# Six tiles instead of seven turned and added by DMA in a residual GNN kernel, the seventh on TensorE, with writes, loads and GpSimd's scaling in another order

## What is computed

```python
x = layernorm(x + gnn_with_batchnorms(x, adj))       # two linear layers, batch statistics
h = relu(adj @ (x @ Wg0 + bg0))                      # per batch
h = relu(adj @ (h @ Wg1 + bg1))
for p in (1, 2, 3, 4):                               # windows of p rows of the 128
    wins = h[:, :nw * p, :].reshape(B * nw, p, H)    # nw = 128 // p
    last = lstm_last(Wih[p-1], Whh[p-1], bih[p-1], bhh[p-1], wins)
    h = h.at[:, arange(nw) * p + (p - 1), :].set(last.reshape(B, nw, H))
x = layernorm(x + h)
```

## Time and profile before

| what | value |
|---|---|
| median of 3 runs | 751.12 us (750.57 to 752.2) |
| the profiled execution, its own time | 748.24 us |
| span of its profile | 746.4 us |
| TensorE's granted clock over the span | 0.995 |
| TensorE, VectorE, ScalarE, GpSimd busy | 97%, 86%, 72%, 42% |

### The profile page before, as it was taken

The page is one execution under the profiler, slowest core; times in us unless marked ns, Lnnn a source line. Parts: engine busy times, 40 slices in busy tenths (PEclk is TensorE's granted clock), DMA queues, the critical chain, the costliest instruction groups (busy, mean ns, idle before and its releaser), DMA issues.

```text
span 746.4 us, 11167 instructions
## 1 busy us (share of the span) xinstructions
PE 726.6 (97%) x3828; PEld 414.8 (56%) x3828; DVE 644.1 (86%) x1379; ACT 540.2 (72%) x882; POOL 315.2 (42%) x289
## 2 busy tenths in 40 slices
PE   8999999999999999998999999999999999999894
PEld 6777544677777776773444444444444444554442
DVE  6888787899998989857998788899998888888987
ACT  4878998567777776748887787777767766676582
POOL 1000000168788787810000001028287385996286
PEclk9999999999999999999999999999999999999998
DMA  5643400024424233113400006051743526519012
GB/s 158 187 139 97 113 1 0 1 62 109 113 58 114 70 101 89 55 29 146 192 1 2 0 11 117 0 101 50 134 109 74 119 51 141 142 28 215 27 57 84
DMA packets 95291, 61.56 MB, mean 82 GB/s; under 512 B 25178, under 2 KB 94212, under 8 KB 94212
## 3 DMA queue, kind: packets, MB, share of 16 engines
q1 hardware_dynamic: 87844, 49.84, 23.7%
q0 software_dynamic: 7392, 11.01, 7.5%
HBM read 27.55 MB, written 16.78 MB: 59 GB/s over the span
## 4 chain that ended last, share of the span: by engine, by line
PE 60%; DVE 21%; ACT 7%; DMA 4%; SPq 3%; issue 3%; POOL 0%; POOLq 0%; DVEq 0%
PE ps L739 8%; PE ps L740 8%; PE ps L748 8%; PE ps L707 7%; PE ps L744 5%; PE ps L753 5%; PE ps L745 5%; ACT work L979 4%; PE ps L646 4%; DVE ln_stats L1263 3%; SPq L510 3%; DVE work L1227 2%; DVE store L1291 2%; DVE ring L1244 2%; DVE ring L1280 2%
## 5 line engine op out<-in xcount | busy, mean ns | idle before, releaser
L979 ACT ACTIVATE work<-ps,gate_bias 128x512 f32<-128x512 f32 x449 | 280.9, 679 | 78.7 <-PE ps L753 44.8
L739 PE MATMUL ps<-store,wih 128*128 128x512 f16 (+1 forms) x443 | 166.9, 377 | 2.4 <-ACT work L979 2.3
L740 PE MATMUL ps<-store,wih 128*128 128x512 f16 (+1 forms) x443 | 166.8, 377 | 0.0
L748 PE MATMUL ps<-store,wih 128*128 128x512 f16 (+1 forms) x443 | 156.2, 377 | 0.0
L577 POOL TENSOR_SCALAR ring<-ring,ln_mv 128x128 f32<-128x128 f32 x112 | 112.8, 1018 | 2.8 <-POOL ln_mv L565 2.7
L1227 DVE TENSOR_TENSOR work<-work 128x512 f32<-128x512 f32 (+1 forms) x129 | 88.2, 684 | 22.0 <-ACT work L986 21.9
L986 ACT ACTIVATE work<-store 128x512 f32<-128x512 f32 x97 | 60.5, 624 | 56.3 <-DVE store L1220 41.2
L588 POOL DMA_DIRECT2D ring<-turned x8 | 10.6, 1319 | 198.5 <-DMA turned<-store 190.5
L744 PE MATMUL ps<-store,whh 128*128 128x512 f16 (+1 forms) x248 | 93.3, 376 | 0.0
L745 PE MATMUL ps<-store,whh 128*128 128x512 f16 (+1 forms) x248 | 93.2, 376 | 0.0
L753 PE MATMUL ps<-store,whh 128*128 128x512 f16 (+1 forms) x248 | 93.1, 376 | 0.0
(11 more groups left out here) (140 smaller groups left out, 1274.0 us busy)
## 6 DMA issues: line engine op xcount, KB each, us to landing
ring<-in_x_dram SPq DMA_DIRECT2D x32, 256.0 KB, 2.9
ring<-in_x_dram SPq DMA_DIRECT2D x16, 512.0 KB, 5.2
x_scratch<-ring SPq DMA_DIRECT2D x16, 512.0 KB, 3.5
ring<-turned POOLq DMA_DIRECT2D x8, 768.0 KB, 6.3
ring<-x_scratch SPq DMA_DIRECT2D x5, 1024.0 KB, 6.4
store<-turned POOLq DMA_DIRECT2D x6, 768.0 KB, 6.8
out_dram<-ring SPq DMA_DIRECT2D x5, 768.0 KB, 3.9
store<-x_scratch SPq DMA_DIRECT2D x3, 1024.0 KB, 14.2
```

The costliest lines, as they stand in the source:

```text
L739: nc.tensor.matmul(acc(j), w_hi, x_hi, start=True, stop=False)
L740: nc.tensor.matmul(acc(j), w_lo, x_hi, start=False, stop=False)
L748: last = nc.tensor.matmul(acc(j), weights(wih, j)[0], x_lo, start=False, stop=u.first)
L979: nc.scalar.activation(acts[:, n % 2, gate, 0:u.cols], ps[:, gate_bank(q), 0:u.cols], ACT.Tanh if gate == G else ACT.Sigmoid, bias=gate_bi ...
```

## The change

Tile 6 leaves `MOVED`: its rows 0 to 2 are turned on TensorE and added on VectorE as tile 7's are, at units 116 to 118 (`TURNS`) and 117 to 119 (`STATS`); before, its statistics stood at 119, 120 and 121, the last together with row 0 of tile 7. ScalarE's scaling of tile 6 moves from behind units 123 to 125 to behind 121 to 123. The moves of tiles 0 to 5 keep their unit numbers; in `move_rows` the high half waits for the high halves of h and for the first add of the tile before, and only the low half for the rest. GpSimd issues the low half's add one unit behind the high half's, and the scaling of a moved tile's rows stands in three parts at one to three units (`PARTS`). A write may stand behind the next move (`WRITES`). The load of tiles 6 and 7 has one wait more.

```diff
-MOVED = range(P // T_TILE - 1)
+MOVED = range(P // T_TILE - 2)
...
-        wanted.append((start + (STATS_DELAY if tile < MOVED[-1] else ROWS_ADDED) - 1, tile))
+        wanted.append((start + (STATS_DELAY if tile < 6 else ROWS_ADDED) - 1, tile))
...
-OUT_DELAY = 4
...
+def scale_slots():
+    parts = {}
+    for n in sorted(MOMENTS):
+        for piece in MOMENTS[n]:
+            if piece in POOLED:
+                for k, r in enumerate(moment_rows(piece)):
+                    later = (0, 1, 3)[k] if piece[0] + 1 in MOVED else 0
+                    parts.setdefault(n + later, []).append((piece, r))
+    return parts
...
+def write_slots():
+    slots = {}
+    move_of = {tile: n for n in MOVES for tile in MOVES[n]}
+    for n in sorted(MOMENTS):
+        for tile, r in MOMENTS[n]:
+            at = n + (3 if r == 3 else 4)
+            if r == 0 and move_of.get(tile + 2, at) <= n + 7:
+                at = max(at, move_of.get(tile + 2, at))
+            slots.setdefault(at, []).append((tile, r))
+    return slots
...
             def move_rows(tile):
                 n = MOVE_ORDER.index(tile)
-                sp.wait_ge(lo_done, halves_through(max(NUMBER[v] for v in sources(Unit(4, tile, 0)))))
-                wait(sp, h_added, 32 * n)
-                for s in range(2):
+                for s, done in enumerate((hi_done, lo_done)):
+                    sp.wait_ge(done, halves_through(max(NUMBER[v] for v in sources(Unit(4, tile, 0)))))
+                    wait(sp, h_added, 16 * (2 * n - 1 + s) if n else 0)
...
                     sp.wait_ge(out_written[tile % X1_RING], 32 * (tile // X1_RING + 1))
+                    sp.wait_ge(h_added, 32 * (len(MOVED) - 1))
                     load_x1(tile + X1_RING)
...
-            for n in range(N_EARLY, len(UNITS) + OUT_DELAY):
+            for n in range(N_EARLY, max(WRITES) + 1):
                 for tile in MOVES.get(n, ()):
                     move_rows(tile)
-                for piece in MOMENTS.get(n - OUT_DELAY, ()):
+                for piece in WRITES.get(n, ()):
                     write_rows(piece)
...
             for n in range(N_EARLY, len(UNITS)):
                 for tile in LANDS.get(n, ()):
-                    add_rows(tile)
+                    add_rows(tile, 0)
+                for tile in LANDS.get(n - 1, ()):
+                    add_rows(tile, 1)
+                for piece, r in PARTS.get(n, ()):
+                    if piece not in MOMENTS.get(n, ()):
+                        scale_row(piece, r)
                 for piece in MOMENTS.get(n, ()):
-                    scale_rows(piece)
+                    raise_rows(piece)
+                    for part, r in PARTS.get(n, ()):
+                        if part == piece:
+                            scale_row(piece, r)
```

More of the change, by code:

```diff
@@ L215 @@
 TAIL = MOMENTS[len(UNITS) - 1]
+def scale_slots():
[17 more added lines that the diff above has]
+    return slots
 def moment_rows(piece):
     return range(0, 3) if piece[1] == 0 else range(3, 4)
+PARTS, WRITES = scale_slots(), write_slots()
 def resnorm_gnn_kernel(nc, x, adj, W1, b1, g1, be1, W2, b2, g2, be2,
@@ L579, in _, with add_rows @@
                 last.then_inc(x1_ready, 1)
-            def add_rows(tile):
+            def add_rows(tile, s):
                 n = MOVE_ORDER.index(tile)
@@ L584, in add_rows, with raise_rows @@
                 pool.wait_ge(x1_loaded[tile % X1_RING], 16 * (tile // X1_RING + 1))
[L585 to L590, removed]
+                pool.wait_ge(h_moved[s], 16 * CB * (n + 1))
+                wait(pool, h_added, 16 * (2 * n + s))
+                nc.gpsimd.dma_start(rows, h_rows[:, s, :, :].rearrange("p (m r) d -> p m (r d)", r=3),
+                                    accum_op=ALU.add).then_inc(h_added, 16)
+            def raise_rows(piece):
                 n = MOMENT_ORDER.index(piece)
@@ L597, in scale_rows, with scale_row @@
                     .then_inc(end_rstd, 1)
-                if piece in BY_VECTOR:
-                    return
+                if piece in BY_SCALARE:
+                    pool.wait_ge(end_step, 4 * (n + 1))
+                    pool.wait_ge(end_rstd, n + 1)
+                    nc.gpsimd.tensor_tensor(mv[:, 2, cols], mv[:, 1, cols], mv[:, 4, cols], ALU.mult)\
+                        .then_inc(end_offset, 1)
+            def scale_row(piece, r):
+                n, tile = MOMENT_ORDER.index(piece), piece[0]
+                mv = end_mv[:, tile, :, :]
@@ L600, in scale_rows @@
                 pool.wait_ge(end_step, 4 * (n + 1))
                 pool.wait_ge(end_rstd, n + 1)
[L602 to L611, removed]
@@ L612, in scale_rows @@
-                last.then_inc(end_scaled, 1)
+                for m in range(CB):
+                    row = x1_tile[tile % X1_RING][:, 4 * m + r, :]
+                    k = r * CB + m
+                    last = nc.gpsimd.tensor_scalar(row, row, mv[:, 1, k:k + 1], mv[:, 4, k:k + 1],
+                                                   ALU.subtract, ALU.mult)
+                if r == moment_rows(piece).stop - 1:
+                    last.then_inc(end_scaled, 1)
             for n in range(N_EARLY, len(UNITS)):
```

## The result

| | median | range | runs |
|---|---|---|---|
| before | 751.12 us | 748.62 to 752.79 | 9 |
| with the change | 747.32 us | 747.10 to 747.60 | 9 |

The ratio is 0.9956, its 95% interval 0.9942 to 0.9969: 3.8 us or half a per cent faster, and outside the range of 748.2 to 752.0. The sign of the sum was right, its size was not: -0.7 us had been forecast.

A forecast was written before the change was run, and what follows sets the result against it. TensorE was taken to set the pace from 350 to 700 us. Turns of +1.35 us and the closed hole of -2.14 gave -0.79, taken as -0.7: 750.4 us at the median, range 748.2 to 752.0.

The forecast's parts named there:

- TensorE gets 3 x 8 = 24 matmuls: Tile 6's turns on TensorE around units 116 to 118: 0.45 us per 8, all on the path, +1.35 us.
- Rival D: The turning matmuls on TensorE cost their listed 0.22 us each, 5.3 us less 2.14: 754.3 us; chance 0.01.
- the 6.6 us of the prediction's other reading of this price: The 24 turns on TensorE at the Trainium skill page's about 275 ns each: 6.6 us against the 1.35 taken.
- The whole hole of 2.14 us closes: TensorE's hole from 700.04 us, before the turn behind unit 122, goes because hidden(121) is ready by 701.39: -2.14 us.
- the walk through VectorE and ScalarE: Reckoning of units 117 to 121: hidden(119) 0.84 us later, hidden(121) starting at about 700.6 us and ending at 701.3.
- Rival B: VectorE is late at unit 121 by its own work, the hole stays and shifts: +2.2 us, 753.3; chance 0.08.
- The first waits for the add of tile 3's row 3: Tile 6's first turn needs a bank free at 670.52 us; TensorE comes at 671.14, 0.6 us to spare: cost 0.
- The other moves: Transposing DMAs of tiles 2, 4 and 5 start sooner, VectorE's waits of 0.3 and 1.1 us go: 0 us gained.
- -2.14 us: Size given to closing TensorE's hole from 700.04 to 702.18 us at the turn behind unit 122.
- Rival A: Tile 6's hole is longer in timed runs, holding the whole 2.88 us: 747.5 us; chance 0.25 for over 1.5 us gain.
- I take 0.1: GpSimd's last chain, 717.81 to 739.16 us, may keep 0.1 to 0.5 us of the gain; 0.1 us was taken.
- Rival C: GpSimd's last chain holds the end if tile 7's moments come 0.8 us later: no gain, 751.1 us; chance 0.15.

The follow-up runs named there:

- the pair of runs: Kernel before with two pieces of SyncE's queue placed otherwise, tile 6 turned on TensorE against tile 6 moved, one chip: 747.20 against 745.87 us.
- the long profile: The kernel before, unchanged, profiled again: this profiled execution took 752.79 us, span 751.0; its 12 runs had a median of 751.11 us.
- the one with the late move: Tile 6's move held for one more unit's low half, against the kernel before with two pieces of SyncE's queue placed otherwise: 753.08 us, ratio 1.0034.

## Why the prediction was wrong, point by point

- *"TensorE gets 3 x 8 = 24 matmuls"*, +1.35 us: right, 1.33 by the pair of runs. In the profile after, the 8 of tile 6's first row stand between 671.12 and 671.57, 0.45 us. Rival D, 0.22 us each, has fallen. So has the 6.6 us of the prediction's other reading of this price.
- *"The whole hole of 2.14 us closes"*: right, with 0.8 us more to spare than the walk through VectorE and ScalarE gave: hidden(121) starts at 699.77, where 700.6 had been reckoned. By starts the hole is 2.30 us, and 1.35 - 2.30 = -0.95 is what the two spans show (-1.0). Rival B has fallen: hidden(119) is as late as it was, 691.98, and not 0.84 later.
- *"The first waits for the add of tile 3's row 3 ... 0.6 us to spare; Cost 0"*: right, TensorE's first turn of tile 6 starts at 671.12 without a hole.
- *"The other moves ... The two short waits of VectorE for such adds (0.3 and 1.1 us) go ... All of that is under TensorE's solid stretch: 0."* **This is the step that failed.** It was 0 in the execution that was profiled, and the sum was then carried over to the median of the runs as if the runs were like it. Tile 5's wait was on the edge there: 1.1 us is absorbed, 3.8 us is not. In the two long executions that were profiled it is 3.8 and 4.1 us, and it costs 2.4 to 2.6 us at the end, in 44 of the 78 runs of the kernel before. Tile 6 alone on TensorE left that cost in (749.76); another place of one write took it out (745.69 against 747.99).
- *"-2.14 us"* for the hole at unit 122 was sized by its shortest form. With the clock's fall behind it it cost 4.6 us in the long profile. 1.35 less the full costs of a long execution, 2.5 + 2.8 + 1.75, is -5.7; less the hole of a short one alone, -0.95. The median of before, 751.12, lies where the heap with tile 5's holes and the full clock lies (its nine runs have no clock on record): 1.35 - 2.3 - 2.5 = -3.5, and -3.8 was measured. So the clock, which falls in 43 of the 78 runs, widens the spread of before but adds little to this difference of medians.
- *Rival A* saw that the 2.88 us between the profiled execution and the median might stand in the DMA chain, and its 747.5 is nearly what came out (747.32). That is luck in part. It named one of two places, and the one that varied less: tile 6's wait differed by 0.5 us between the two profiles, tile 5's by 2.7. The clock's fall behind tile 6's hole, which does vary, was in no term. Rival A was given 0.25, with nothing to tie the 2.88 us to a place; the range left out its price of 747.5.
- *"I take 0.1"* for GpSimd's last chain, and *Rival C*: nothing was kept; the span fell by 1.0 us, as much as TensorE gained. The chain does come closer. It works from 717.45 to its power for tile 6's row 3 at 738.66 without the two pauses, as foreseen, and starts that power 0.50 us sooner than the 739.16 of the earlier trace rows, where TensorE's last turn comes 0.99 us sooner. But its very last power, tile 7's, still waits for VectorE, 0.66 us where it had been 1.16:

```profile
717.45 2.67 POOL L625 TENSOR_TENSOR end_mv<-end_mv,minus_half 128x12 f32<-128x12 f32 x1 [0.26 <-DVE end_mv L1297]
...
738.66 1.02 POOL L625 TENSOR_TENSOR end_mv<-end_mv,minus_half 128x4 f32<-128x4 f32 x1
740.35 1.06 POOL L625 TENSOR_TENSOR end_mv<-end_mv,minus_half 128x4 f32<-128x4 f32 x1 [0.66 <-DVE end_mv L1297]
```

**What stays open.** Why tile 5's chain comes in two forms. In the short one (the first profile) GpSimd's 12 scalings of tile 3 take 13.11 us and the last transposing DMA lands in 3.38 us, in the long one 13.92 and 5.59; which sets off which was not tried. Nor is it known why the clock falls in some executions of the kernel before and not in others; that needs profiles of the two heaps that have none.

## What to carry to other kernels

When one profiled execution is shorter than all timed runs, it does not show what the median holds: compare its time with the spread first, and treat each short wait for a DMA in it as a candidate for the missing time, also where the bounding engine shows no hole. Ask of every wait how much longer it could get before the engine that sets the pace stands still. Before work is given back to the engine that sets the pace, look at what the late transfer shares its time with; here one write one unit sooner and one write behind a move gave some 5 us at no cost, and tile 6 on TensorE on top of that costs 1.3 of it again.

## What was not expected of the hardware

- **An adding DMA beside a load.** The low add of 768 KB lands 5.7 to 5.9 us after its issue with no load or write issued in the two microseconds behind it, 9.3 to 9.4 with a load of 1 MB issued behind it, and 11.65 and 11.80 with that load and a write of 768 KB. The order in SyncE's queue decided which it was.
- **A short hole can cost more than its length.** TensorE's granted clock stayed at 1.00 behind the hole of 2.30 us at unit 122 and was 0.57 over the 4 us that followed holes of 2.83 and 4.49 us, with matmuls at half pace until 708.7 and 708.4; 1.6 to 1.75 us on top of the hole. In the kernel before the mean clock was 0.993 or less in 43 of 78 runs, in the one with the late move in all 10, and in the kernels whose profiles have no hole at unit 122 in none of 78.
